# A recommender's forward pass: sixteen gathers fetched by SP and ACT row by row, and all of ACT's copies moved to DVE

## The reference

```python
x = relu(dense_features @ W0 + b0)
x = relu(x @ W1 + b1)
dense_out = relu(x @ W2 + b2)
emb = vmap(lambda t, idx: t[idx], in_axes=(0, 1), out_axes=1)(tables, sparse_features)
gram = einsum('bid,bjd->bij', emb, emb)
interact = gram[:, TRIU_I, TRIU_J]
return concatenate([dense_out, interact], axis=1) @ Wt + bt
```

## Time and profile before

| | |
|---|---|
| profiled execution | 537.25 us |
| its span (first to last instruction) | 535.4 us |
| PE busy | 352.0 us, 66% |
| PEld busy | 289.4 us, 54% |
| DVE busy | 207.0 us, 39%, 648 instructions |
| ACT busy | 204.2 us, 38%, 637 instructions |
| POOL busy | 396.4 us, 74%, 424 instructions |
| mean share of the granted TensorE clock | 0.784 |
| a gather, from issue to landing, median | 2.7 us |
| DVE's clear of w_tri (L330), once | 5.4 us |
| mlp_l1 of one round, begin to end | 3.64 us |
| DMA engines busy | 18.2% of 16 engines for the gathers, 1.9% for SP's queue |

### The profile page before, as it was taken

How to read it: one execution, slowest core, us unless ns; L and a number is a source line. 1 busy time by engine, 2 the same in 40 slices (tenths; PEclk the granted TensorE clock), 3 DMA queues, 4 the chain that set the end, 5 groups by cost and what they waited for, 6 DMA issues and landing times.

```text
span 535.4 us, 8028 instructions
## 1 busy us (share of the span) xinstructions
PE 352.0 (66%) x1744; PEld 289.4 (54%) x1744; DVE 207.0 (39%) x648; ACT 204.2 (38%) x637; POOL 396.4 (74%) x424
## 2 busy tenths in 40 slices
PE   2159774585666864868547958369556686677865
PEld 1148663475555753657436746258444575465644
DVE  5633433444314444233444343243431443413533
ACT  2134522454315443244443453245431544414622
POOL 5777777777777777777777777777777777777773
PEclk9975876878867877668877697687985878766979
DMA  5224122221122122221222211222112211122111
GB/s 104 32 47 89 28 29 37 36 29 28 27 38 38 28 27 28 39 38 28 28 32 32 38 28 28 38 38 28 26 28 38 38 27 27 26 38 36 28 23 30
DMA packets 21563, 18.82 MB, mean 35 GB/s; under 512 B 11028, under 2 KB 14870, under 8 KB 21496
## 3 DMA queue, kind: packets, MB, share of 16 engines
q0 software_dynamic: 13472, 13.63, 18.2%
q1 hardware_dynamic: 4544, 2.41, 1.9%
q10 hardware_dynamic: 3498, 2.26, 1.4%
HBM read 15.34 MB, written 2.10 MB: 33 GB/s over the span
## 4 chain that ended last, share of the span: by engine, by line
POOL 72%; issue 23%; PE 2%; DVE 1%; DMA 1%; POOLq 0%
POOL emb L275 72%; PE mlp_ps L572 1%; DVE gram L199 1%; DMA emb<-in_L_rec_tables_dram,row_idx 1%; DMA raw_idx<-n_r_sparse_features_dram 0%; PE gram_ps L559 0%; POOLq L79 0%; PE rowsT_ps L542 0%; POOLq L272 0%; DVE out_sb L372 0%; DVE embT L185 0%; DVE wrap L311 0%; DVE wrapped L315 0%; DVE row_idx L321 0%; DVE capped L312 0%
## 5 line engine op out<-in xcount | busy, mean ns | idle before, releaser
L275 POOL DMA_INDIRECT emb<-in_L_rec_tables_dram,row_idx x410 | 387.2, 944 | 128.5 <-issue 124.7
L199 ACT COPY gram<-gram_ps 32x48 f32<-32x48 f32 (+1 forms) x512 | 122.9, 240 | 149.0 <-PE gram_ps L559 143.1
L199 DVE COPY gram<-gram_ps 32x48 f32<-32x48 f32 (+1 forms) x512 | 121.9, 238 | 124.8 <-PE gram_ps L559 117.9
L542 PE MATMUL rowsT_ps<-ident,emb 128*128 128x128 f32 (+1 forms) x218 | 51.6, 345 | 161.2 <-DMA emb<-in_L_rec_tables_dram,row_idx 143.9
L559 PEld LDWEIGHTS gram_ps<-embT 128*128 128x128 f32 x1024 | 144.7, 229 | 17.4 <-issue 9.4
L559 PE MATMUL gram_ps<-embT 128*128 128x100 f32 x1024 | 148.7, 313 | 4.1 <-DVE embT L185 4.1
L542 PEld LDWEIGHTS rowsT_ps<-ident,emb 128*128 128x128 f32 (+1 forms) x218 | 28.8, 164 | 181.5 <-DMA emb<-in_L_rec_tables_dram,row_idx 144.2
L185 DVE COPY embT<-rowsT_ps 64x512 f32<-64x512 f32 (+2 forms) x96 | 65.4, 690 | 150.3 <-PE rowsT_ps L542 149.9
L185 ACT COPY embT<-rowsT_ps 64x512 f32<-64x512 f32 x64 | 53.8, 864 | 113.4 <-PE rowsT_ps L542 113.0
L572 PE MATMUL mlp_ps<-w_gram,gram 128*128 128x256 f32 x224 | 76.6, 508 | 2.0 <-DVE gram L199 2.0
L572 PEld LDWEIGHTS mlp_ps<-w_gram,gram 128*128 128x128 f32 x224 | 60.4, 274 | 15.5 <-DVE gram L199 2.3
(11 more groups left out here) (29 smaller groups left out, 39.8 us busy)
## 6 DMA issues: line engine op xcount, KB each, us to landing
by_hand<-in_L_rec_tables_dram SPq DMA_DIRECT2D x768, 0.2 KB
emb<-in_L_rec_tables_dram,row_idx POOLq DMA_INDIRECT x410, 2.7
out_dram<-out_sb ACTq DMA_DIRECT2D x16, 128.0 KB, 1.9
w_gram<-w_tri SPq DMA_DIRECT2D x3, 192.0 KB
w_sb<-in_L_rec_W_dram SPq DMA_DIRECT2D x1, 512.0 KB
raw_idx<-n_r_sparse_features_dram SPq DMA_DIRECT2D x2, 182.0 KB, 4.2
w_gram<-w_tri SPq DMA_DIRECT2D x1, 224.0 KB
spare<-in_L_rec_tables_dram,row_idx POOLq DMA_INDIRECT x7, 2.7
```

The lines of the kernel that those rows point to most:

```text
L199: last = copy(gram[FP * g:FP * (g + 1), q, t0:NS, c0 + a0 * SQ + s:c0 + a1 * SQ:SQ], gram_ps[FP * s:FP * (s + 1), a0:a1, src:src + SQ * (N ...
L275: nc.gpsimd.indirect_dma_start(emb[:, j, k, :], None, tables_v[:, :], bass.IndirectOffsetOnAxis(ap=row_idx[:, r * UR + j, k:k + 1], axis=0 ...
L542: last = nc.tensor.transpose(rowsT_ps[BANK[c]][0:m * EMB, (k - 8 * BANK[c]) // 2, :, :], by_hand[:, bass.ds(r - R_SP, 1), :] if own else e ...
```

## The change

Three things are changed together.

1. Sixteen gathers, the thirteenth of the units 4, 7, 10, ... 28 (nine, on SP) and 5, 9, 14, 17, 21, 26, 30 (seven, on ACT), are fetched row by row. GpSimd issues 400 gathers, and the seven spare ones are gone. A TENSOR_LOAD brings 32 offsets in place of 16, these are in bytes already (DVE multiplies by 256), and the table is addressed as bytes, which leaves the register multiplication out. Each unit has a buffer and a semaphore of its own, so SP no longer waits between units. SP fetches the first 64 rows of unit 4 ahead of the four w_gram copies. ACT fetches 32 rows per unit of the program, between the stores.
2. DVE takes over what ACT did: the odd tables' copies to embT, all gram copies, and the relus, as tensor_scalar (add the bias, maximum with 0). Only in the very last unit ACT still copies.
3. The gram copies wait for the whole unit and then take it in 16 copies of 96 or 112 elements, where DVE had 16 and ACT 16 of 48 or 56.

DVE also clears w_tri earlier, so SP's w_tri loads begin ahead of where they did.

```diff
-    R_SP = 2
-    N_SP = ROUNDS - R_SP
-    LOADED = 16
-    PROBES = [128, 127, 124, 120, 64, 32, 16]
+    SP_UNITS = [4, 7, 10, 13, 16, 19, 22, 25, 28]
+    ACT_UNITS = [5, 9, 14, 17, 21, 26, 30]
+    BY_HAND = SP_UNITS + ACT_UNITS
+    LOADED = 32
+    ROW = EMB * 4
...
-    tables_flat = tables.rearrange("f v e -> (f v e)")
+    tables_bytes = tables.rearrange("f v e -> (f v e)").bitcast(mybir.dt.uint8)
...
+        def fetch_rows(eng, n, first, stop):
+            i, at = BY_HAND.index(n), n % 2 * NP + n // 2
+            for c0 in range(first, stop, LOADED):
+                _, offs = nc.values_load_multi_w_load_instructions(
+                    hand_off[at:at + 1, c0:c0 + LOADED], engines=[eng.engine], min_val=0,
...
+                for c, off in enumerate(offs, c0):
+                    row = c % 2 * US + c // 2
+                    eng.dma_start(by_hand[row:row + 1, i, :].bitcast(mybir.dt.uint8),
+                                  tables_bytes[bass.ds(off, ROW)].rearrange("(a e) -> a e", a=1)
+                                  ).then_inc(by_hand_in[i], 16)
...
@@ SP @@
+            sp.wait_ge(hand_idx_ready, 1)
+            fetch_rows(sp, SP_UNITS[0], 0, 64)
             sp.wait_ge(tri_in, 16 * (F - 1))
...
-            for i in range(N_SP):
...
-                sp.wait_ge(by_hand_in, 16 * P * (i + 1))
+            fetch_rows(sp, SP_UNITS[0], 64, P)
+            for n in SP_UNITS[1:]:
+                fetch_rows(sp, n, 0, P)
@@ GpSimd @@
+                for c, ks in enumerate(CHUNKS):
+                    if c == LAST and r * UR + j in BY_HAND:
+                        continue
...
-            for i, n in enumerate(PROBES):
-                nc.gpsimd.indirect_dma_start(
...
@@ VectorE @@
             nc.vector.memset(ident[:, :], 0.0).then_inc(zeros_set, 1)
+            nc.vector.memset(w_gram[:, 0, :], 0.0)
             for part, (u0, u1) in enumerate(PARTS):
+                if part == 1:
+                    nc.vector.memset(w_tri[:, :, :], 0.0).then_inc(tri_zeroed, 1)
...
                     rowsT_evac(nc.vector.tensor_copy, c, 0, j).then_inc(embT_even[c], 1)
+                    if n != LAST_UNIT and len(CHUNKS[c]) > 1:
+                        rowsT_evac(nc.vector.tensor_copy, c, 1, j).then_inc(embT_odd[c], 1)
             def gram_blocks(r, j):
...
-                for half in range(2):
-                    dve.wait_ge(gram_in_psum, (r * UR + j) * 2 + half + 1)
-                    gram_evac(nc.vector.tensor_copy, DVE_BLOCKS, j, half).then_inc(gram_evac_dve, 1)
+                dve.wait_ge(gram_in_psum, (r * UR + j) * 2 + 2)
+                gram_evac(nc.vector.tensor_copy, BLOCKS, j, 0, NG).then_inc(gram_ready, 1)
...
+            def relu(out, in_, bias):
+                return nc.vector.tensor_scalar(out, in_, bias, 0.0, ALU.add, ALU.max)
...
+            def vector_round(r):
+                embT_evac(r, 0)
+                if r > 0:
+                    out_evac(r - 1, 1)
+                gram_blocks(r, 0)
+                embT_evac(r, 1)
+                l0_evac(r)
+                gram_blocks(r, 1)
+                l1_evac(r)
+                embT_evac(r, 2)
+                l2_evac(r)
+                gram_blocks(r, 2)
+                embT_evac(r, 3)
+                out_evac(r, 0)
+                if r == ROUNDS - 1:
+                    gram_blocks_tail()
+                else:
+                    gram_blocks(r, 3)
@@ ScalarE: scalar_round and what it calls go @@
+            pieces = [(n, c0) for n in ACT_UNITS for c0 in range(0, P, LOADED)]
+            act.wait_ge(hand_idx_ready, 1)
+            for n in range(NU):
+                r, j = n // UR, n % UR
+                if r > 0 and j % 2 == 0:
+                    store(r - 1, j // 2)
+                for unit, c0 in pieces[n:n + 1]:
+                    fetch_rows(act, unit, c0, c0 + LOADED)
@@ TensorE @@
                 pe.wait_ge(embT_even[LAST], n + 1)
                 pe.wait_ge(embT_odd[LAST - 1], n + 1)
+                wait_if_any(pe, gram_ready, n)
                 for half in range(2):
-                    wait_if_any(pe, gram_evac_dve, (n - 1) * 2 + half + 1)
-                    wait_if_any(pe, gram_evac_act, (n - 1) * 2 + half + 1)
```

216 lines of the change are left out of this document (83 added, 133 removed).

## The result

The changed kernel takes 607.57 us (median of 4 runs, 607.24 to 608.12) against 537.24 before: a ratio of 1.130, 95% interval 1.129 to 1.132. The forecast was slower, 558 us, at most 582. The sign and the mechanism were right, the size was not: 49 us too little. One execution in all, the profiled one of the run with one chunk ahead, was a slow one (562.76 us), and its time is in no median and no ratio.

What follows compares the result with a forecast made beforehand. DVE's copies and TensorE's products in turn bound the kernel at 66.9 us per round, over 62.4 of gathers; unit 31's last transpose at 541.7, plus 14.9 tail and 1.85 outside the span, gives 558.4 us, range 529 to 582.

Steps and rivals of the forecast that it cites:

- The ring: DVE's copies and TensorE's products alternating through every unit: 66.9 us per round against 62.4 of gathers; chance 0.60.
- Its pieces: Per unit, gram copies 5.36 us, four embT copies 3.18, plus last transpose, evacuation, copy and handovers: 9.87 us.
- The line of 161 ns and 1.6 ns per element: DVE copy cost fitted to five traced sizes; gives 315 and 340 ns for gram copies of 96 and 112 elements.
- I take the mixture of before: TensorE's clock stays as before: a round's products take 3.71 + 5.71 + 3.81 + 3.81 = 17.0 us.
- 72.7 us per round for four slow units: Round length if all four units' products took 5.71 us at TensorE's slower clock; no separate chance given.
- The sum: Round of the four units: 39.5 + 17.0 + 5.9 + 3.1 + 0.5 + 0.9 = 66.9 us.
- one us per round moves this by 7.5: Sensitivity of the forecast time: each us more or less per round shifts it by 7.5 us.
- Between nothing and some 2 us: At the start, delay of the first landing because w_tri loads share DMA engines with unit 0's gathers.
- the formula for unit 1 (39.6): Unit 1's last gather, the 26th, starts at 5.41 + 25 x 1.249 = 36.6; its last transpose is at 39.6.
- SP's rows: 128 rows take SP 48.7 to 53.7 us, deciding only above 51.6 per unit; SP late means 578 us, chance 0.18.
- ACT without cost: ACT's 32 rows per unit take 12 to 14 us in units of 16.7, so no cost.
- The tail: From the last unit's last transpose to the span's end: steps kept as before, 14.9 us.

Runs made afterwards that it cites:

- the run with one chunk ahead: The changed kernel, with the next unit's chunk 0 transposed before a unit's products and copied by DVE beside them: 554.83 us, ratio 1.0289.
- the larger dose: The changed kernel, with TensorE repeating first-chunk transposes 10, 10, 4, 2 times and second-chunk ones 14, 14, 14, 18 times per round's units, same result: 553.01 us.
- the later rows: The changed kernel without SP and ACT row fetches in the first two units (fourteen units, 402 gathers), early clear kept: 602.27 us, ratio 1.1189.

## Why the prediction was wrong in size

- **The ring becomes the bound: right.** The waits asked for are there, the gathers went from 95% of the chain to 12% at most (POOL and issue), and opening the ring brings the gathers' bound back.
- **Its pieces.** Forecast 9.87 us per unit for copies and handovers. Measured about 10.0: gram copies 5.48 (5.36), embT copies 3.28 (3.18), the rest as read from before. Over four units that is 0.6 more. The line of 161 ns and 1.6 ns per element held (323 and 354 ns for 315 and 340). By the Trainium skill's price for a copy out of PSUM (VectorE: DVE Perf Modes, TRN2 errata) the two are estimated at 225 and 242 ns, which would have kept the gathers as the bound; these copies, at 323 and 354 ns, contradict it for this strided form.
- **"I take the mixture of before": this step failed.** It is the term for TensorE's clock. The round's products were put at 17.0 us and measured 3.71 + 6.29 + 5.65 + 6.30 = 21.95, 4.9 more; 0.8 of it is that the one round read before was a short one (17.9 in the mean). The prediction had called the clock its softest part and named 72.7 us per round for four slow units, but kept the old mixture although it had just shown that the pauses change. The run with the larger dose shows that filling the pauses brings the clock back (0.939 for 0.775) and 54.6 us with it; which of the pauses matter stayed open. mlp_l2 is the same term: 1.97 us for 1.08, 0.9 more. top went the other way: 5.10 us from start to products for 6.44, 1.3 less. With the later rows the products were 20.64 and top 6.43, in a round of the same length: the term that failed is the clock of all of TensorE's stages in the ring, some 4.5 us a round, and not that of the products alone.
- **The sum**: 66.9 + 4.9 + 0.9 - 1.3 + 0.6 = 72.0, measured 71.68. The 4.8 us per round are 36 us in all, by "one us per round moves this by 7.5".
- **"Between nothing and some 2 us" for the start: this step failed too.** It was 13.0: 5.6 by the clear, of which 4.4 are the held-up gather (most of the rest is that the first gather started at 5.96 and not at 5.31), 6.2 by the rows beside the first gathers, and 1.2 that the formula for unit 1 (39.6) lay below the kernel before (40.81). That DVE's clear can hold up a gather was in no row of before, where it ran later and held up nothing; that some 180 row fetches of SP and ACT run beside the gathers of the first 60 us followed from the diff, and had no term.
- **SP's rows: right, but by a narrow margin.** They came 51.0 us apart, under the deciding 51.6 of the forecast ring. The ring that came out gave them 53.8. The load of 32 offsets took 2.18 us on SP and 2.31 on ACT, near the upper end; the estimate of 1.86 from the Trainium skill's floor (DMA: Bandwidth & Descriptors, Latency and other measured facts) was too low, and a row was a little cheaper than 0.334 us.
- **ACT without cost: right** in the rounds, not at the start.
- **The tail**: 606.2 - 590.04 = 16.2 us for 14.9: the last products took 5.44 us instead of 3.81.
- **The range.** Its upper end, 582, allowed for the ring at 69 per round and for SP late. All products slow, 72.7 per round, was written down and then given no weight; by the prediction's own 7.5 us per us of round it is 602 us.

## What to carry to other kernels

When a change makes an engine wait in a place where it did not, its clock is a term of the sum with its own two ends, not a constant: price every stage of that engine at both levels and put both in the range. Here all slow against the mixture was 5.8 us of a round, more than the 4.5 by which the ring was put above the gathers. An engine that is off the chain (here DVE, 39% busy before) becomes part of a ring when its work moves from beside the products to behind them. Moving it back beside them, one unit ahead, opened the ring. And of an edit at the start, ask both what runs at the same moment and what waits behind it: the early clear held a gather up by 4.4 us and let SP start eleven us sooner.
